# Two last products of a two-group matmul chain, each done in seven products of half the size

## The chip, the cores and the metric

The program runs on one core of a Trainium2 chip. The metric is the device time of one execution in microseconds (us). The core's engines work in parallel and are ordered by semaphores alone: TensorE (PE) multiplies, VectorE (DVE) and ScalarE (ACT) work element by element, GpSimd (POOL) and SyncE (SP) issue transfers here.

## The reference

For eight sequences of 256 tokens with 1024 features, one of eight square matrices is chosen for each sequence and applied; then a dense layer with a gated low-rank part is applied, and the input is added to the result:

```
xc  = einsum('bsi,boi->bso', x, weight[ids])             # 8 x 256 x 1024, one 1024 x 1024 matrix each
combine = top-2 of softmax(xc @ W_router.T), scaled to sum 1
h   = einsum('nd,erd->ner', xc, A_stack) * combine[..., None]
out = x + xc @ W_base.T + b_base + einsum('ner,eor->no', h, B_stack) * 2.0
```

## The kernel before, in words

**Two halves, high and low.** Each float32 operand is split in two fp32r values: ScalarE casts it (the high part, helper `hi`, line 492), VectorE subtracts the cast from the original (the low part, helper `lo`, line 553). A product is then three matmuls for each 128x128 block of weights (`product`, lines 813 to 815): high by high, high by low, low by high.

**Groups.** The sequences go in two groups of four. In each group the first part makes `xc` (`cond`, lines 828 and 832: 8 tiles of 128 outputs for a sequence). The second part multiplies all four sequences' `xc`, seen as a matrix of 1024 rows by 1024 tokens, by `W_base`. That product is done in seven products of half the size (P1, P2, P5, P6, P7, P4, P3, in this order in `second`), each of 512 outputs by 512 k by 512 tokens: four tiles m of 128 outputs, four k steps, three matmuls of 512 columns each. The sums that this needs of quarters of `W_base` (`s_sum`) and of `xc` (`t_sum`) are VectorE's (line 557), in place. P2, P7, P4 and P3 also take the low-rank part in (`lora_up`, three more matmuls to a tile).

**Banks and passes.** The eight accumulators are `bank_x0` to `bank_x3` and `bank_y0` to `bank_y3`. After a product VectorE adds a bank to the output in `out_sb` (`first_pass`, line 596; `last_pass`, line 604), and the next product goes on accumulating in the same bank; so TensorE waits for VectorE's pass of tile m before it writes the bank again (`wait_bank`, `cond_bank`). The output quarters are named t1/C11, t2/C12, t3/C22 and C21. P3 ends C12; it accumulates in `bank_y`, and in the second group its last tile is cut in two halves of 256 columns (`end_tile`, `end_passes`, line 612), so that the last pass and the last store are short.

**What sets the order.** Every engine has its own instruction list, written out by hand in program order, and does it strictly in that order. VectorE's list for the end of a group is in the loop over groups: passes, low parts for P3's weights, low parts of the next group's first `x` and `w` tiles. ScalarE's list is `base_splits`. SP issues the loads of `raw`'s six slots in a fixed order (`load_order`); each waits until the slot's former content has been used (`wait_free`), and what stands behind it waits too. POOL issues the loads of the residual `x` and all stores but the last.

## Time and profile before

| | us |
|---|---|
| median of 3 runs | 394.96 |
| lowest, highest | 394.69, 395.39 |
| the profiled execution's own time | 394.37 |
| its span, first to last instruction | 392.6 |

| engine | busy us | share of the span |
|---|---|---|
| TensorE matmul | 388.7 | 99% |
| TensorE weight load | 332.8 | 85% |
| VectorE | 302.0 | 77% |
| ScalarE | 183.6 | 47% |
| GpSimd | 50.0 | 13% |

A busy share tells how much of the span an engine had something to do. It is a mean over stages, and says nothing of the place where an engine is waited for. Of a matmul the profile gives start and a modelled duration that overlaps the next one; the pace is read from the distance of starts.

### The profile page before, as it was taken

The page shows a single profiled execution, that of the slowest core. Times are in us where ns is not written, and L with a number is a line of the kernel's source. Part 1 is how long each engine was busy: PE and PEld are TensorE (multiplying, and loading weights), DVE is VectorE, ACT ScalarE, POOL GpSimd, SP SyncE. Part 2 cuts the span into 40 slices and gives each one's busy share as a digit, 9 for nine tenths or more (in the row PEclk, how much of TensorE's full clock was granted, in tenths as well). Part 3 has the DMA queues.
Part 4 walks back from the last instruction along what each step waited for, and adds up shares of the span by engine and source line. Part 5 has one row for each costly group of instructions (what it writes and reads, how often), then busy time and mean ns, then how long its engine had stood idle before and what let it go on. Part 6 is the DMA issues. An engine that isn't in the chain of part 4 may idle for free.

```text
span 392.6 us, 5707 instructions
## 1 busy us (share of the span) xinstructions
PE 388.7 (99%) x2185; PEld 332.8 (85%) x2185; DVE 302.0 (77%) x431; ACT 183.6 (47%) x281; POOL 50.0 (13%) x84
## 2 busy tenths in 40 slices
PE   8999999999999999999999999999999999999997
PEld 8888888888888888888888888888888888888886
DVE  4897966789699999974458786778867989998322
ACT  5877734758632444232147666357656224441000
POOL 0101103110002130021130000260000202201110
PEclk9999999999999999999999999999999999999999
DMA  7997875869333145586668767489083302552222
GB/s 263 391 361 281 291 269 125 283 224 334 119 107 27 56 157 169 179 279 206 215 222 275 229 230 251 117 246 387 29 264 117 72 5 81 182 167 80 82 80 80
DMA packets 21979, 73.95 MB, mean 188 GB/s; under 512 B 3344, under 2 KB 3600, under 8 KB 21952
## 3 DMA queue, kind: packets, MB, share of 16 engines
q1 hardware_dynamic: 15984, 55.58, 41.5%
q0 software_dynamic: 5680, 16.96, 14.3%
q10 hardware_dynamic: 288, 1.05, 0.7%
q8 instruction: 17, 0.28, 0.3%
q14 instruction: 10, 0.08, 0.1%
HBM read 64.13 MB, written 8.39 MB: 185 GB/s over the span
## 4 chain that ended last, share of the span: by engine, by line
PE 99%; DVE 0%; issue 0%
PE bank_x L828 30%; PE bank_x L832 16%; PE bank_y L813 9%; PE bank_y L815 9%; PE bank_y L814 8%; PE bank_x L815 8%; PE bank_x L814 8%; PE bank_x L813 8%; PE bank_y L883 2%; PE bank_y L959 2%; DVE out_sb L612 0%; DVE h_hl L549 0%
## 5 line engine op out<-in xcount | busy, mean ns | idle before, releaser
L828 PE MATMUL bank_x<-x_hl,wc_hl 128*128 128x512 f32 x512 | 123.3, 391 | 0.0
L553 DVE TENSOR_TENSOR wc_hl<-raw,wc_hl 128x1024 fp32r<-128x1024 f32 x90 | 108.4, 1220 | 18.5 <-ACT wc_hl L492 18.3
L492 ACT CAST wc_hl<-raw 128x1024 fp32r<-128x1024 f32 x90 | 93.6, 1051 | 56.1 <-DVE raw L557 22.9
L828 PEld LDWEIGHTS bank_x<-x_hl,wc_hl 128*128 128x128 f32 x512 | 94.1, 189 | 18.0
L832 PEld LDWEIGHTS bank_x<-x_hl,wc_hl 128*128 128x128 f32 x512 | 65.9, 191 | 2.6
L832 PE MATMUL bank_x<-x_hl,wc_hl 128*128 128x256 f32 x512 | 66.7, 283 | 0.0
L521 ACT COPY xc_low<-bank_x 128x256 f32<-128x256 f32 x64 | 23.7, 370 | 33.7 <-PE bank_x L832 21.9
L706 DVE TENSOR_TENSOR xp<-bank_x,xc_low 128x256 f32<-128x256 f32 x64 | 26.9, 421 | 15.2 <-ACT xc_low L521 14.1
L814 PE MATMUL bank_x<-x_hl,wc_hl 128*128 128x512 f32 x96 | 37.4, 389 | 0.0
L815 PE MATMUL bank_x<-x_hl,wc_hl 128*128 128x512 f32 x96 | 37.4, 389 | 0.0
L813 PE MATMUL bank_x<-x_hl,wc_hl 128*128 128x512 f32 x96 | 37.4, 389 | 0.0
L526 ACT CAST xc_hl<-xp 128x256 fp32r<-128x256 f32 x64 | 26.0, 406 | 24.0 <-DVE xp L706 23.9
L596 DVE SCALAR_TENSOR_TENSOR out_sb<-bank_x,bias_sb,out_sb 128x512 f32<-128x512 f32 x32 | 23.6, 747 | 17.4 <-PE bank_x L815 15.1
L711 DVE TENSOR_TENSOR xc_hl<-xp,xc_hl 128x256 fp32r<-128x256 f32 x64 | 26.9, 420 | 7.5 <-ACT xc_hl L526 7.5
L431 POOL DMA_DIRECT2D out<-out_sb x28 | 15.4, 550 | 124.1 <-DVE out_sb L604 102.1
L425 POOL DMA_DIRECT2D out_sb<-x x32 | 22.9, 720 | 56.1 <-PE bank_x L828 55.9
L604 DVE TENSOR_TENSOR out_sb<-bank_y,out_sb 128x512 f32<-128x512 f32 x23 | 15.7, 688 | 15.1 <-PE bank_y L815 14.3
L440 POOL DMA_DIRECT2D gate_rows<-compared x16 | 9.6, 612 | 132.1 <-DVE compared L679 132.1
L492 ACT CAST x_hl<-xp 128x1024 fp32r<-128x1024 f32 x16 | 16.6, 1051 | 15.1 <-DVE xp L557 14.7
L814 PE MATMUL bank_y<-xc_hl,wc_hl 128*128 128x512 f32 x60 | 23.4, 389 | 0.0
L813 PE MATMUL bank_y<-xc_hl,wc_hl 128*128 128x512 f32 x60 | 23.4, 389 | 0.0
L815 PE MATMUL bank_y<-xc_hl,wc_hl 128*128 128x512 f32 x60 | 23.4, 389 | 0.0
(88 smaller groups left out, 505.5 us busy)
## 6 DMA issues: line engine op xcount, KB each, us to landing
raw<-w_cond SPq DMA_DIRECT2D x62, 512.0 KB, 4.7
raw<-w_base SPq DMA_DIRECT2D x24, 512.0 KB, 5.2
out_sb<-x POOLq DMA_DIRECT2D x32, 256.0 KB, 4.7
raw<-x SPq DMA_DIRECT2D x14, 512.0 KB, 4.8
out<-out_sb POOLq DMA_DIRECT2D x28, 256.0 KB, 2.3
raw<-x ACTq DMA_DIRECT2D x2, 512.0 KB, 3.7
raw<-w_cond SPq DMA_DIRECT2D x4, 256.0 KB, 3.5
gate_rows<-compared POOLq DMA_DIRECT2D x16, 64.0 KB, 3.9
```

The lines of the kernel that those rows point to most:

```text
L492: nc.scalar.copy(split_dst(key, HI), split_src(key)).then_inc(hi_done, 1)
L521: nc.scalar.copy(xc_low[:, t % 2], bank_x[t % HT][:, TOK:]).then_inc(low_copied, 1)
L526: nc.scalar.copy(xc_hl[:, t, HI, s % 2 * TOK:(s % 2 + 1) * TOK], xp[:, s // 2 % 2, t, s % 2 * TOK:(s % 2 + 1) * TOK]).then_inc(xc_hi, 1)
L553: nc.vector.tensor_tensor(split_dst(key, LO), split_src(key), split_dst(key, HI).bitcast(F32), ALU.subtract).then_inc(lo_done, 1)
L596: nc.vector.scalar_tensor_tensor(out_sb[:, o], bank_x[m][:], bias_sb[:, i:i + 1], out_sb[:, o], ALU.add, ALU.add).then_inc(pass_done, 1)
L706: nc.vector.tensor_tensor(xc, bank_x[t % HT][:, 0:TOK], xc_low[:, t % 2], ALU.add) \
L711: nc.vector.tensor_tensor(xc_hl[:, t, LO, s % 2 * TOK:(s % 2 + 1) * TOK], xc, xc_hl[:, t, HI, s % 2 * TOK:(s % 2 + 1) * TOK].bitcast(F32), ...
L813: nc.tensor.matmul(ps, w_hi, v_hi, start=start, stop=False, skip_group_check=resumed)
L814: nc.tensor.matmul(ps, w_hi, v_lo, start=False, stop=False, skip_group_check=resumed)
L815: return nc.tensor.matmul(ps, w_lo, v_hi, start=False, stop=stop, skip_group_check=resumed)
L828: return nc.tensor.matmul(ps[:], wc_hl[:, slot_of(s, t), HI, k], x_hl[:, s % 2, k].rearrange("p h n -> p (h n)"), start=(k == 0), stop=stop)
L832: return nc.tensor.matmul(ps[:, TOK:], wc_hl[:, slot_of(s, t), LO, k], x_hl[:, s % 2, k, HI], start=False, stop=stop)
```

## The change

In both groups P3 is itself done in seven products of 256 outputs by 256 k by 256 tokens. They are called P1 to P7 again, with their operands U (weights) and V (`xc`); TensorE does them in `third` in the order P1, Y, P6, P5, P7, P3, P4. A tile of one has two k steps and three matmuls each, all of 256 columns, and each of the seven has two tiles; P2's two tiles are the first part of Y0 and Y1. Y0 to Y3 are the low-rank part of the four tiles of C12 (three matmuls of 512 columns each, as before). P1, P6, P7 and P4 accumulate in `bank_x0/1`, P5 and P3 in `bank_x2/3`, Y in `bank_y`.

VectorE makes four sums for U and four for V (`u_sum`, `v_sum`, 512 elements to a partition each), the low parts of seven U and four V (512 elements each; three V are quarters of an operand that is split already), and adds every stage's bank to C12 (`inner_passed`: twelve passes of 256 columns, four of 512). ScalarE makes the eleven high parts. The low and high parts of P3's weights (two of 1024 elements each) go, and so do P3's four passes of 512 columns and `end_tile`. The new list of VectorE is `last_stages`. The next group's first matmuls wait for the passes of the inner P4 and P3 now, and before waited for those of C21; the loads of two `raw` slots for the next group's third and fourth `w` tiles wait for inner sums and splits.

The diff, cut to its core:

```diff
+INNER = [(P1, "t1"), ("Y", "Y"), (P6, "t2"), (P5, "C22"), (P7, "t3"), (P3, "C12"), (P4, "C21")]
+INNER_TILES = [(j, m) for j, _ in INNER for m in range(HT if j == "Y" else HT // 2)]
+INNER_W = {P1: (0, 0), P2: (0, 1), P4: (1, 1)}
+INNER_X = {P1: (0, 0), P2: (1, 0), P3: (1, 1)}
+U_SUMS, V_SUMS = (P5, P6, P7, P3), (P5, P6, P7, P4)
+U_PLACE = (P1, P2, P6, P5, P7, P3, P4)
...
-            P7: s(P4), P4: s(P3) + ([] if last else [("x", n, 0), ("x", n, 1)]),
-            P3: [] if last else [("w", n, 0), ("w", n, 1), ("w", n, 2), ("w", n, 3)]}
+            P7: s(P4),
+            P4: [("U", g, P1), ("U", g, P2)] + ([] if last else [("x", n, 0), ("x", n, 1)]) +
+                [("V", g, P6), ("U", g, P6), ("V", g, P5), ("U", g, P5), ("V", g, P7)],
+            P3: [("U", g, P7), ("U", g, P3), ("V", g, P4), ("U", g, P4)] +
+                ([] if last else [("w", n, 0), ("w", n, 1), ("w", n, 2), ("w", n, 3)])}
...
+        def w_quarter(r, c):
+            return raw[:, R1 + r].rearrange("p (m k n) -> p m k n", m=2, k=HT)[:, :, 2 * c:2 * c + 2]
+        def x_quarter(r, c):
+            return xp[:, 1, HT + 2 * r:HT + 2 * r + 2, c * TOK:(c + 1) * TOK]
...
-                elif kind in ("A11", "A12", "A22", "A22b"):
-                    j = {"A11": P7, "A12": P2, "A22": P3, "A22b": P4}[kind]
+                elif kind == "A22":
+                    sp.wait_ge(summed, SUM["U", g, P3])
+                    sp.wait_ge(lo_done, SPLIT["U", g, P4 if h else P2])
+                elif kind in ("A11", "A12", "A22b"):
...
+                if kind == "U":
+                    q = U_PLACE.index(j)
+                    act.wait_ge(product_done, made(i, P7, q // 2 * 2 + 1) if q < 4 else made(i, P4, HT - 1))
+                if kind == "V":
+                    act.wait_ge(product_done, made(i, P7, HT - 1))
...
+            def u_sum(g, j):
+                dve.wait_ge(summed, SUM["U", g, {P6: P5, P3: P6}[j]] if j in (P6, P3) else SUM["S", g, (P3, 1)])
+                a, b, op = {P5: (w_quarter(1, 0), w_quarter(1, 1), ALU.add),
+                            P6: (u_plain(P5), w_quarter(0, 0), ALU.subtract),
+                            P7: (w_quarter(0, 0), w_quarter(1, 0), ALU.subtract),
+                            P3: (w_quarter(0, 1), u_plain(P6), ALU.subtract)}[j]
+                total(u_plain(j), a, b, op)
+            def v_sum(g, j):
+                if j in (P6, P4):
+                    dve.wait_ge(summed, SUM["V", g, {P6: P5, P4: P6}[j]])
+                a, b = {P5: (x_quarter(0, 1), x_quarter(0, 0)), P6: (x_quarter(1, 1), v_plain(P5)),
+                        P7: (x_quarter(1, 1), x_quarter(0, 1)), P4: (x_quarter(1, 0), v_plain(P6))}[j]
+                total(v_plain(j), a, b, ALU.subtract)
...
+            def inner_passed(g, j, m):
+                o = OUT_SLOT["C12"]
+                if (j, m) in ((P1, 0), (P1, 1), ("Y", 2), ("Y", 3)):
+                    dve.wait_ge(pass_done, passed(g, "t2", m))
+                else:
+                    dve.wait_ge(inner_pass, {"Y": inner(g, P1, m % 2), P6: inner(g, "Y", m % 2),
+                                             P5: inner(g, "Y", 2 + m % 2), P7: inner(g, P5, m % 2),
+                                             P3: inner(g, P6, m % 2), P4: inner(g, "Y", 2 + m % 2)}[j])
+                dve.wait_ge(inner_done, inner(g, j, m))
+                if j == "Y":
+                    dst, ps = out_sb[:, o + m], bank_y[m][:]
+                else:
+                    c = 0 if j in (P1, P4) else TOK
+                    dst = out_sb[:, o + m + (0 if j in (P1, P6, P3) else 2), c:c + TOK]
+                    ps = bank_x[m + (2 if j in (P5, P3) else 0)][:, 0:TOK]
+                nc.vector.tensor_tensor(dst, ps, dst, ALU.add).then_inc(inner_pass, 1)
+            def last_stages(g):
+                def los(*keys):
+                    for key in keys:
+                        lo(key)
+                n = GSEQS * (g + 1)
+                last = g == GROUPS - 1
+                los(("U", g, P1))
+                first_pass(g, "t3", 3)
+                last_pass(g, "C22", 3)
+                los(("U", g, P2))
+                first_pass(g, "C21", 0)
+                if not last:
+                    los(("x", n, 0), ("x", n, 1))
...
+                if not last:
+                    los(("w", n, 1))
+                for m in range(2):
+                    inner_passed(g, P7, m)
+                for m in range(2):
+                    inner_passed(g, P3, m)
+                if not last:
+                    los(("w", n, 2))
+                for m in range(2):
+                    inner_passed(g, P4, m)
+                if not last:
+                    los(("w", n, 3))
...
-                        pe.wait_ge(pass_done, passed(s // GSEQS - 1, "C21", t))
+                        pe.wait_ge(inner_pass, inner(s // GSEQS - 1, P4 if t < 2 else P3, t % 2))
...
+            def inner_tile(g, j, m, ps, resumed):
+                pe.wait_ge(lo_done, SPLIT["U", g, j])
+                if j not in INNER_X:
+                    pe.wait_ge(lo_done, SPLIT["V", g, j])
+                for k in range(2):
+                    mm = product(ps, u_split(g, j, HI)[:, m, k], u_split(g, j, LO)[:, m, k], v_split(j, HI)[:, k],
+                                 v_split(j, LO)[:, k], not resumed and k == 0, k == 1, resumed=resumed)
+                return mm
+            def third(g):
+                for j, m in INNER_TILES:
+                    if j == "Y":
+                        pe.wait_ge(pass_done, passed(g, "C22", m))
+                        if m < 2:
+                            inner_tile(g, P2, m, bank_y[m][:, 0:TOK], True)
+                        mm = lora_up(bank_y[m][:], KT + m, 1)
+                    else:
+                        b = m + (2 if j in (P5, P3) else 0)
+                        if j in (P1, P5):
+                            pe.wait_ge(pass_done, passed(g, "C21", b))
+                        else:
+                            pe.wait_ge(inner_pass, inner(g, {P6: P1, P7: P6, P4: P7, P3: P5}[j], m))
+                        mm = inner_tile(g, j, m, bank_x[b][:, 0:TOK], j not in (P1, P5))
+                    mm.then_inc(inner_done, 1)
```

VectorE's list from the end of P7 to the end of group 0, before (L553 low parts, L596 and L604 passes; the rows of `x_hl` and the last rows of `wc_hl` are the next group's):

```order
L553 TENSOR_TENSOR wc_hl<-raw,wc_hl 128x1024 [waits hi_done]
L596 SCALAR_TENSOR_TENSOR out_sb<-bank_x0,bias_sb,out_sb 128x512 [waits res_in0,product_done]
L553 TENSOR_TENSOR x_hl<-raw,x_hl 128x4x256 [waits hi_done] x2
L596 SCALAR_TENSOR_TENSOR out_sb<-bank_x1,bias_sb,out_sb 128x512 [waits res_in1,product_done]
L596 SCALAR_TENSOR_TENSOR out_sb<-bank_x2,bias_sb,out_sb 128x512 [waits res_in2,product_done]
L596 SCALAR_TENSOR_TENSOR out_sb<-bank_x3,bias_sb,out_sb 128x512 [waits res_in3,product_done]
L553 TENSOR_TENSOR wc_hl<-raw,wc_hl 128x1024 [waits hi_done] x2
L604 TENSOR_TENSOR out_sb<-bank_y0,out_sb 128x512 [waits pass_done,product_done]
L604 TENSOR_TENSOR out_sb<-bank_y1,out_sb 128x512 [waits pass_done,product_done]
L553 TENSOR_TENSOR wc_hl<-raw,wc_hl 128x1024 [waits hi_done]
L604 TENSOR_TENSOR out_sb<-bank_y2,out_sb 128x512 [waits pass_done,product_done]
L604 TENSOR_TENSOR out_sb<-bank_y3,out_sb 128x512 [waits pass_done,product_done]
```

The same place now, its first twelve rows (L627 are sums, L623 low parts, L666 C21's passes; `xp` holds the new sums):

```order
L666 SCALAR_TENSOR_TENSOR out_sb<-bank_x0,bias_sb,out_sb 128x512 [waits res_in0,product_done]
L623 TENSOR_TENSOR x_hl<-raw,x_hl 128x4x256 [waits hi_done] x2
L627 TENSOR_TENSOR xp<-xp 128x512
L627 TENSOR_TENSOR xp<-xp 128x512 [waits summed]
L627 TENSOR_TENSOR xp<-raw 128x512 [waits summed]
L627 TENSOR_TENSOR xp<-xp,raw 128x512 [waits summed]
L666 SCALAR_TENSOR_TENSOR out_sb<-bank_x1,bias_sb,out_sb 128x512 [waits res_in1,product_done]
L623 TENSOR_TENSOR x_hl<-xp,x_hl 128x512 [waits hi_done]
L623 TENSOR_TENSOR wc_hl<-xp,wc_hl 128x512 [waits hi_done]
L627 TENSOR_TENSOR xp<-xp 128x512
L627 TENSOR_TENSOR xp<-xp 128x512 [waits summed]
L666 SCALAR_TENSOR_TENSOR out_sb<-bank_x2,bias_sb,out_sb 128x512 [waits res_in2,product_done]
```

Between two of C21's passes, where nothing or one low part stood, there are now three to six instructions.

The end of VectorE's list for group 0 now (L709 are `inner_passed`; the rows of `wc_hl` with 1024 elements are the next group's weights; the first `bank_x0/1` pair is P7's, the second P4's, `bank_x2/3` are P5's and P3's):

```order
L623 TENSOR_TENSOR wc_hl<-raw,wc_hl 128x1024 [waits hi_done]
L709 TENSOR_TENSOR out_sb<-bank_x2,out_sb 128x256 [waits inner_done,inner_pass]
L709 TENSOR_TENSOR out_sb<-bank_x3,out_sb 128x256 [waits inner_done,inner_pass]
L623 TENSOR_TENSOR wc_hl<-raw,wc_hl 128x1024 [waits hi_done]
L709 TENSOR_TENSOR out_sb<-bank_x0,out_sb 128x256 [waits inner_done,inner_pass]
L709 TENSOR_TENSOR out_sb<-bank_x1,out_sb 128x256 [waits inner_done,inner_pass]
L709 TENSOR_TENSOR out_sb<-bank_x2,out_sb 128x256 [waits inner_done,inner_pass]
L709 TENSOR_TENSOR out_sb<-bank_x3,out_sb 128x256 [waits inner_done,inner_pass]
L623 TENSOR_TENSOR wc_hl<-raw,wc_hl 128x1024 [waits hi_done]
L709 TENSOR_TENSOR out_sb<-bank_x0,out_sb 128x256 [waits inner_done,inner_pass]
L709 TENSOR_TENSOR out_sb<-bank_x1,out_sb 128x256 [waits inner_done,inner_pass]
L623 TENSOR_TENSOR wc_hl<-raw,wc_hl 128x1024 [waits hi_done]
```

The four low parts of the next group's weights stand between the inner passes, three of them ahead of P4's.

TensorE's list at the boundary of P4 and P3 in group 0, before:

```order
L813 MATMUL bank_x3<-h_hl,b_hl 128x512
L814 MATMUL bank_x3<-h_hl,b_hl 128x512
L815 MATMUL bank_x3<-h_hl,b_hl 128x512
L813 MATMUL bank_y0<-xc_hl,wc_hl 128x512 [waits pass_done,lo_done]
L814 MATMUL bank_y0<-xc_hl,wc_hl 128x512
L815 MATMUL bank_y0<-xc_hl,wc_hl 128x512
L813 MATMUL bank_y0<-xc_hl,wc_hl 128x512
L814 MATMUL bank_y0<-xc_hl,wc_hl 128x512
L815 MATMUL bank_y0<-xc_hl,wc_hl 128x512
```

TensorE's list at the boundary of group 0 and group 1, now (L933 to L935 are the inner P4, L948 and L952 the next group's first tiles):

```order
L933 MATMUL bank_x1<-x_hl,xc_hl 128x256 [waits lo_done,inner_pass]
L934 MATMUL bank_x1<-x_hl,xc_hl 128x256
L935 MATMUL bank_x1<-x_hl,xc_hl 128x256
L933 MATMUL bank_x1<-x_hl,xc_hl 128x256
L934 MATMUL bank_x1<-x_hl,xc_hl 128x256
L935 MATMUL bank_x1<-x_hl,xc_hl 128x256
L948 MATMUL bank_x0<-x_hl,wc_hl 128x512 [waits lo_done,inner_pass,hi_done]
L948 MATMUL bank_x0<-x_hl,wc_hl 128x512 x7
L948 MATMUL bank_x1<-x_hl,wc_hl 128x512 [waits inner_pass,hi_done]
L952 MATMUL bank_x0<-x_hl,wc_hl 128x256 [waits lo_done]
L952 MATMUL bank_x0<-x_hl,wc_hl 128x256 x7
```

The tile that follows P3 on TensorE now waits for `inner_pass`, a pass of the product just done, where it waited for passes of C21 that had been done a stage earlier.

## Rows read from the trace of the kernel before

**Rows 1.** The page: busy time, and the chain that ended last.

```profile
PE 388.7 (99%) x2185; PEld 332.8 (85%) x2185; DVE 302.0 (77%) x431; ACT 183.6 (47%) x281; POOL 50.0 (13%) x84
PE 99%; DVE 0%; issue 0%
```

**Rows 2.** Windows of group 0's P4 and P3: us, busy us of each engine (instructions).

```profile
171.10:184.70 13.60, 13.60 (x61) 11.27 (x60) 7.09 (x8) 4.01 (x4) 2.17 (x4) 1.00 0.81 290
184.70:198.30 13.60, 13.60 (x61) 11.27 (x60) 6.32 (x7) 2.10 (x2) 2.16 (x4) 1.00 0.58 194
```

**Rows 3.** Timeline, PE: start us, us, what; group 1's P3, then group 0's end.

```profile
375.93 0.39 PE L813 MATMUL bank_y<-xc_hl,wc_hl 128*128 128x512 f32 x1
...
386.13 0.28 PE L813 MATMUL bank_x<-xc_hl,wc_hl 128*128 128x256 f32 x1
...
389.60 0.28 PE L815 MATMUL bank_x<-h_hl,b_hl 128*128 128x256 f32 x1
...
198.33 0.84 PE L828 MATMUL bank_x<-x_hl,wc_hl 128*128 128x512 f32 x3
```

**Rows 4.** Timeline, DVE, group 0's P4 and P3 ([idle before it <- ended by]).

```profile
172.79 1.22 DVE L553 TENSOR_TENSOR wc_hl<-raw,wc_hl 128x1024 fp32r<-128x1024 f32 x1
174.73 0.75 DVE L596 SCALAR_TENSOR_TENSOR out_sb<-bank_x,bias_sb,out_sb 128x512 f32<-128x512 f32 x1 [0.72 <-PE bank_x L815]
175.39 2.35 DVE L553 TENSOR_TENSOR x_hl<-raw,x_hl 128x1024 fp32r<-128x1024 f32 x2
178.13 0.75 DVE L596 SCALAR_TENSOR_TENSOR out_sb<-bank_x,bias_sb,out_sb 128x512 f32<-128x512 f32 x1 [0.38 <-PE bank_x L815]
181.53 0.75 DVE L596 SCALAR_TENSOR_TENSOR out_sb<-bank_x,bias_sb,out_sb 128x512 f32<-128x512 f32 x1 [2.65 <-PE bank_x L815]
184.93 0.75 DVE L596 SCALAR_TENSOR_TENSOR out_sb<-bank_x,bias_sb,out_sb 128x512 f32<-128x512 f32 x1 [2.65 <-PE bank_x L815]
...
198.53 0.69 DVE L604 TENSOR_TENSOR out_sb<-bank_y,out_sb 128x512 f32<-128x512 f32 x1 [2.71 <-PE bank_y L815]
```

**Rows 5.** Timeline, DVE, a busy stretch of group 0's P2: independent instructions.

```profile
132.03 1.28 DVE L604 TENSOR_TENSOR out_sb<-bank_y,out_sb 128x512 f32<-128x512 f32 x2
133.23 2.35 DVE L557 TENSOR_TENSOR xp<-xp 128x1024 f32<-128x1024 f32 x2
135.50 0.68 DVE L604 TENSOR_TENSOR out_sb<-bank_y,out_sb 128x512 f32<-128x512 f32 x1
```

**Rows 6.** Timeline, DVE: two passes of P1, then the next instruction.

```profile
125.51 1.40 DVE L596 SCALAR_TENSOR_TENSOR out_sb<-bank_x,bias_sb,out_sb 128x512 f32<-128x512 f32 x2
126.83 0.68 DVE L618 TENSOR_TENSOR h_sb<-h_sb,gate_rows 128x512 f32<-128x512 f32 x1
```

**Rows 7.** Timeline, DVE, 256 elements: a dependent pair, then an independent pair.

```profile
115.50 0.43 DVE L662 TENSOR_TENSOR compared<-compared,const_sb 128x256 f32<-128x256 f32 x1
115.97 0.43 DVE L664 TENSOR_TENSOR compared<-compared 128x256 f32<-128x256 f32 x1
...
211.05 0.41 DVE L706 TENSOR_TENSOR xp<-bank_x,xc_low 128x256 f32<-128x256 f32 x1
211.39 1.21 DVE L553 TENSOR_TENSOR wc_hl<-raw,wc_hl 128x1024 fp32r<-128x1024 f32 x1
```

**Rows 8.** Groups by line and shape: busy us, mean ns; idle before, releaser.

```profile
L553 DVE TENSOR_TENSOR xc_hl<-xp,xc_hl 128x1024 fp32r<-128x1024 f32 x8 | 9.4, 1220 | 0.0
L496 ACT CAST h_hl<-h_sb 128x512 fp32r<-128x512 f32 x4 | 2.5, 621 | 16.5 <-DVE h_sb L618 16.5
```

**Rows 9.** Line 394 (SP's loads of `raw`): the time to landing.

```profile
DMA to landing us min/median/max: 3.2/4.9/9.1
```

**Rows 10.** Timeline, DVE, group 1's P4 and P3.

```profile
365.93 0.75 DVE L596 SCALAR_TENSOR_TENSOR out_sb<-bank_x,bias_sb,out_sb 128x512 f32<-128x512 f32 x1 [0.72 <-PE bank_x L815]
...
376.13 0.75 DVE L596 SCALAR_TENSOR_TENSOR out_sb<-bank_x,bias_sb,out_sb 128x512 f32<-128x512 f32 x1 [2.65 <-PE bank_x L815]
...
389.92 0.42 DVE L612 TENSOR_TENSOR out_sb<-bank_x,out_sb 128x256 f32<-128x256 f32 x1 [1.30 <-PE bank_x L815]
```

**Rows 11.** The program's start: PE timeline (the warm-up's last ten matmuls), and the page's clock.

```profile
4.78 2.33 PE L959 MATMUL bank_y<-h_hl 128*128 128x256 f32 x10
...
PEclk9999999999999999999999999999999999999999
```

More of the change, by code:

```diff
@@ L191 @@
 PASSES = [("t1", m) for m in range(HT)] + [("C11", m) for m in range(HT)] + [("t2", m) for m in range(HT)] + \
-    [(c, m) for m in range(HT) for c in ("t3", "C22")] + [("C21", m) for m in range(HT)] + \
-    [("C12", m) for m in range(HT)]
+    [(c, m) for m in range(HT) for c in ("t3", "C22")] + [("C21", m) for m in range(HT)]
 def passed(g, c, m):
@@ L285, in build @@
         stored = [sem(f"stored{i}") for i in range(OUTS)]
-        end_clear = sem("end_clear")
-        end_done = sem("end_done")
-        end_pass = sem("end_pass")
-        end_stored = [sem(f"end_stored{m}") for m in range(HT - 1 + len(END))]
+        inner_done = sem("inner_done")
+        inner_pass = sem("inner_pass")
+        end_stored = [sem(f"end_stored{n}") for n in range(6)]
         block = ctx.enter_context(nc.Block())
@@ L329, in split_src @@
             kind, i, j = key
+            if kind in ("U", "V"):
+                return u_plain(j) if kind == "U" else v_plain(j)
             if kind == "T":
@@ L395, in _ @@
                 in_slot[slot] = key
-            g = GROUPS - 1
-            for m in range(HT - 1):
-                sp.wait_ge(pass_done, passed(g, "C12", m))
-                nc.sync.dma_start(out[2 * g + 1, m], out_sb[:, OUT_SLOT["C12"] + m]).then_inc(end_stored[m], 16)
-            m = HT - 1
-            for n, (a, b) in enumerate(END):
-                sp.wait_ge(end_pass, n + 1)
-                nc.sync.dma_start(out[2 * g + 1, m, :, a:b], out_sb[:, OUT_SLOT["C12"] + m, a:b]) \
-                    .then_inc(end_stored[m + n], 16)
+            g, o = GROUPS - 1, OUT_SLOT["C12"]
+            ends = [(P7, 0, 2, TOK, PTOK), (P7, 1, 3, TOK, PTOK), (P3, 0, 0, 0, PTOK), (P3, 1, 1, 0, PTOK),
+                    (P4, 0, 2, 0, TOK), (P4, 1, 3, 0, TOK)]
+            for n, (j, i, m, a, b) in enumerate(ends):
+                sp.wait_ge(inner_pass, inner(g, j, i))
+                nc.sync.dma_start(out[2 * g + 1, m, :, a:b], out_sb[:, o + m, a:b]).then_inc(end_stored[n], 16)
             for o in range(OUTS):
@@ L477, in hi @@
                     act.wait_ge(raw_in[slot], landed)
+                elif kind == "U":
+                    act.wait_ge(summed, SUM["S", i, (P3, 1)])
                 elif kind != "T":
@@ L490, in hi @@
                 if kind == "w" and i and i % GSEQS == 0 and j < 4:
-                    act.wait_ge(product_done, made(i // GSEQS - 1, P4 if j < 2 else P3, 2 * (j % 2) + 1))
+                    before = i // GSEQS - 1
+                    if j < 2:
+                        act.wait_ge(product_done, made(before, P4, 2 * j + 1))
+                    else:
+                        act.wait_ge(inner_done, inner(before, "Y", 1) if j == 2 else inner(before, P5, 1))
                 nc.scalar.copy(split_dst(key, HI), split_src(key)).then_inc(hi_done, 1)
@@ new lines, in last_stages @@
+            def last_stages(g):
[11 more added lines that the diff above has]
+                    los(("x", n, 0), ("x", n, 1))
+                v_sum(g, P5)
+                v_sum(g, P6)
+                u_sum(g, P5)
+                u_sum(g, P6)
+                first_pass(g, "C21", 1)
+                los(("V", g, P6), ("U", g, P6))
+                v_sum(g, P7)
+                v_sum(g, P4)
+                first_pass(g, "C21", 2)
+                u_sum(g, P7)
+                u_sum(g, P3)
+                los(("V", g, P5), ("U", g, P5))
+                first_pass(g, "C21", 3)
+                los(("V", g, P7))
+                for m in range(2):
+                    inner_passed(g, P1, m)
+                los(("U", g, P7), ("U", g, P3))
+                for m in range(HT):
+                    inner_passed(g, "Y", m)
+                los(("V", g, P4), ("U", g, P4))
+                for m in range(2):
+                    inner_passed(g, P6, m)
+                if not last:
+                    los(("w", n, 0))
+                for m in range(2):
+                    inner_passed(g, P5, m)
+                if not last:
+                    los(("w", n, 1))
+                for m in range(2):
+                    inner_passed(g, P7, m)
+                for m in range(2):
+                    inner_passed(g, P3, m)
+                if not last:
+                    los(("w", n, 2))
+                for m in range(2):
+                    inner_passed(g, P4, m)
+                if not last:
+                    los(("w", n, 3))
@@ L877, in router @@
                 if p == 2:
-                    pe.wait_ge(pass_done, passed(0, "C12", HT - 1))
+                    pe.wait_ge(inner_pass, inner(0, "Y", 1))
                 for k in range(KT):
```

106 lines of the change are left out of this document (43 added, 63 removed).

## The prediction

> **What bounds the kernel now.** First the page: TensorE is busy 99% of the span, the chain that ended last is 99% TensorE, and VectorE is busy 77% [rows 1]. Then the windows of the two stages that the change rewrites in group 0: TensorE fills both, 13.60 us each, and VectorE works 7.09 and 6.32 us in them [rows 2]. So 13.79 of 27.2 us are free on VectorE, and the question is whether what the change puts there fits, in the written order. The timeline of VectorE shows where its free time lies: every pass from 174.73 on starts when TensorE delivers, with up to 2.65 us of idle time ahead [rows 4]. TensorE's starts give the paces: from 375.93 to 386.13 it starts 45 matmuls of 512 columns, 0.2267 us each; from 386.13 the 30th of 256 columns starts at 389.60, 29 steps of 0.1197, call it 0.120 us [rows 3]. The second is more than half of the first; a matmul of half the columns is not half price.
>
> **TensorE's work.** Before, P3 takes 48 matmuls of 512 columns and 12 for the low-rank part. Now there are seven products of two tiles, two k steps and three matmuls: 84 of 256 columns, and the same 12.
> - Group 0: 84 x 0.120 = 10.08 in place of 48 x 0.2267 = 10.88 us. Saved: 0.80 us, if TensorE is never made to wait.
> - Group 1, where the last tile is in 256 columns already: before 45 x 0.2267 + 30 x 0.120 = 13.80, now 84 x 0.120 + 12 x 0.2267 = 12.80 us. Saved: 1.00 us.
>
> The new matmuls read other tiles than those of rows 3, but have their form and weight load. The bounds: no cheaper than 0.1197; at the dearest each as dear as a whole row of 0.2267, which nothing suggests. I take 0.120.
> The Trainium skill ("TensorE: Matmul & The Clock Gate", Back-to-back issue gap) gives N/2.4 + 2.5 ns, an estimate of 0.109 and 0.216 us. By it group 1 would save 1.23 us, not 1.00; the trace's paces are both 0.011 us above it, and the trace decides.
>
> **VectorE's prices.** Independent instructions of 512 elements start 0.60 apart (132.03 to 133.23 for two), of 1024 elements 1.135 (133.23 to 135.50 for two) [rows 5]; C21's kind of pass takes 0.66 (125.51 to 126.83 for two) [rows 6]. With 256 elements one follows 0.34 after an independent one, and 0.47 after one that it needs [rows 7]: a dependence adds 0.13. The new sums read with strides. Bounds: as cheap as 0.60, or 0.73 with the dependence's spacing each. Low parts with strided operands take 1220 ns, like the contiguous ones [rows 8, 4]; so 0.60.
>
> **Group 0, VectorE's list from 174.73.** Up to there nothing moves: P7's last pass and the low part at 172.79 (now half as long) are ahead of C21's first pass, which waits for TensorE [rows 4]. From then to the pass of inner P4's first tile the list has:
> - four passes of C21, 4 x 0.66 = 2.64
> - low parts of the next group's `x`, 2 x 1.13 = 2.26
> - 21 of 512 elements: eight sums, nine low parts, four passes Y; 21 x 0.60 = 12.60, and 2 x 0.13 as two sums need the one just ahead
> - ten inner passes of 256, 3.40
> - low parts of three `w` tiles, 3 x 1.135 = 3.40
>
> Together 24.56 us. With no gap this puts P4's first pass at 199.29. Is there no gap? TensorE's inputs to it are early: from 184.73 (13.60 ahead of 198.33, rows 3) P1 ends at 186.2, Y at 190.3, P6 and P5 at 193.2, while VectorE comes to their passes at 187.7, 189.6, 193.2 and 195.0. P7 then waits 0.4 us for P6's pass and P4 a little for P7's, and P4's first tile is ready at about 198.2. ScalarE's casts of 512 elements take 0.62 [rows 8]; the tightest is U of P6: summed at 180.4, cast by 181.1, wanted at 181.6. The `w` tile whose slot the last sum frees (185.3) lands 4.9 us later, at worst 9.1 [rows 9], so it is cast by 195.5, wanted at 198.15. The next slot is freed at 193.3, and SP's later loads stand behind it; they land about 200, wanted after 203. So VectorE's list is closed, and it sets the end.
> TensorE's first matmul of the next group needs that pass: 199.29 + 0.42 + 0.05 = 199.76, where it started at 198.33 [rows 3]. Group 0 loses 1.43 us; its 0.80 us are turned into waits. Nothing gives that back: behind it TensorE is full to the end. What is late next is the last `w` low part (about 201), wanted by TensorE at 207.
>
> **Group 1.** The same list without the 2.26 and the four `w` low parts. From 365.93 it reaches C21's last pass at 376.1, where TensorE delivers it [rows 10]. Y's passes start from 379.2 and then follow TensorE, which from 375.93 is at 377.4 after P1, 381.5 after Y, 384.4 after P5. P6's pass is over at 384, before P7 wants it. No wait: the full 1.00 us. The last pass moves from 389.92 [rows 10] to 388.92. Behind it is as before a store of 256 columns; the four stores ahead of it are 0.72 us apart now. Cost between 0 and 0.3 us of landing; I take 0.
>
> **Sum.** +1.43 - 1.00 = +0.43 us. The profiled execution took 394.37 us, a span of 392.6 and 1.8 around it, 0.59 under the median of 394.96. It becomes 394.80, the median 395.39. A measurement of this kernel can tell about 0.2%, 0.79 us, from no change.
>
> **Rivals.**
> - *VectorE doesn't bind, faster.* If the inner passes come in time, both savings stand: -1.80 us, 393.2. For it: VectorE had 13.79 us free, and the list adds about as much (11 low parts and 8 sums of 0.60, twelve passes of 0.34, less two low parts of 1.13: 13.2). Against: 1.3 us of the free time is ahead of 174.73, and the next group's weights stand ahead of P4's passes. To save anything the 24.56 must shrink below 23.
> - *VectorE's instructions don't close up, slower.* Each pays the dependence's 0.13 where it reads what was just made elsewhere: nine low parts and the four Y passes, 1.7 us, 397.1. It decides from 0.36 us more on the list. For it: rows 7; most of these wait for a semaphore. Against: low parts that wait for one and find it given follow at the independent pace (175.39, two in 2.35) [rows 4]. If every one started only when the one ahead has ended (0.68, 0.43, 0.75, 1.22), the list would be 27.8 us and the time 398.6. The Trainium skill says so ("VectorE: DVE Perf Modes", The DRAIN you can't avoid: the next operation doesn't start before the pipe is empty). Rows 5 speak against it: two of 0.68 take 1.28 together.
> - *TensorE's clock falls in the new waits, slower.* The first matmuls of the program, 256 columns, take 0.23 us each, the 1.2 GHz level, though the page's granted clock reads 9 there too [rows 11]; later ones 0.120. If the waits at 193 to 199.7 brought it back for one pair of tiles, 16 matmuls of each width, that would be +5.5 us, 401. The waits are short and the trace shows none in mid-program, so little speaks for it.
> - *A weight tile lands late* is covered by 2.6 us even at 9.1 us, and counts for nothing.
>
> **How the numbers follow.** The forecast, 395.4, has a chance of 0.53, with a range of its own from 394.9 to 396.2; 0.08 of it is above 0.2%, as gaps only add. VectorE not binding, whole or in part: 0.18, all of it faster. Instructions not closing up, in part or whole: 0.24, slower. The clock: 0.05. So faster 0.18, same 0.45, slower 0.37. The range reaches from 394.0 (most of the first rival is left out, 0.12) to 397.2 (the clock and the case of 398.6 are left out, 0.08).
>
> **What would show it.** In VectorE's timeline of group 0: no idle time from 174.7 to P4's passes at about 199.3, and the first wide matmul of the next group at about 199.8, released by VectorE's inner pass. TensorE idle between the inner products of group 0, not of group 1. Group 1's TensorE from the start of P3 to the last matmul 12.8 us instead of 13.8, its last pass 1.0 us earlier against the start of that stage. Wrong it would be if VectorE's 512-element instructions start other than 0.60 apart, if the 256-column matmuls start other than 0.12 apart, or if the next group starts on time.

## The result

| | us |
|---|---|
| kernel before, median of 11 runs | 394.78 (394.38 to 395.39) |
| changed kernel, median of 11 runs | 395.88 (395.58 to 396.79) |
| ratio | 1.0032, 95% interval 1.0023 to 1.0040 |
| profiled execution of the changed kernel | 396.25, span 394.5 |

The change makes the kernel 1.1 us slower by the medians, 0.9 to 1.6 by the interval. The forecast was +0.43 us, a time of 395.4: right in direction and with 395.88 inside its own band of 394.9 to 396.2, but the change is 2.6 times as large. More than 0.2% slower, as it came out, had been given a chance of 0.37, and "same" 0.45.

The page of the changed kernel, against [rows 1]:

```profile
PE 387.6 (98%) x2242; PEld 333.1 (84%) x2242; DVE 327.8 (83%) x487; ACT 192.0 (49%) x299; POOL 49.9 (13%) x84
PE 91%; DVE 5%; issue 1%; DMA 1%; SPq 1%; ACT 0%; DVEq 0%; ACTq 0%
```

TensorE has 1.1 us less to do and is a smaller part of the chain that ended last; 5% of it are VectorE's now. The windows of the same two stages, against [rows 2] (the second ends where the next group starts):

```profile
171.66:185.26 13.60, 13.60 (x61) 11.26 (x60) 11.94 (x18) 2.91 (x5) 1.79 (x4) 1.00 0.26 101
185.26:200.30 15.04, 13.76 (x97) 12.40 (x95) 15.04 (x29) 6.20 (x8) 1.99 (x4) 1.00 0.52 188
```

In the second VectorE is busy 15.04 of 15.04 us, TensorE 13.76. VectorE's timeline there, against [rows 4]:

```profile
175.29 0.75 DVE L666 SCALAR_TENSOR_TENSOR out_sb<-bank_x,bias_sb,out_sb 128x512 f32<-128x512 f32 x1 [1.26 <-PE bank_x L935]
175.96 2.35 DVE L623 TENSOR_TENSOR x_hl<-raw,x_hl 128x1024 fp32r<-128x1024 f32 x2
178.23 1.42 DVE L627 TENSOR_TENSOR xp<-xp 128x512 f32<-128x512 f32 x2
179.56 0.68 DVE L627 TENSOR_TENSOR xp<-raw 128x512 f32<-128x512 f32 x1
...
181.55 0.68 DVE L623 TENSOR_TENSOR x_hl<-xp,x_hl 128x512 fp32r<-128x512 f32 x1
182.15 0.68 DVE L623 TENSOR_TENSOR wc_hl<-xp,wc_hl 128x512 fp32r<-128x512 f32 x1
182.75 1.29 DVE L627 TENSOR_TENSOR xp<-xp 128x512 f32<-128x512 f32 x2
...
190.15 2.48 DVE L709 TENSOR_TENSOR out_sb<-bank_y,out_sb 128x512 f32<-128x512 f32 x4
...
198.66 1.22 DVE L623 TENSOR_TENSOR wc_hl<-raw,wc_hl 128x1024 fp32r<-128x1024 f32 x1
199.80 0.75 DVE L709 TENSOR_TENSOR out_sb<-bank_x,out_sb 128x256 f32<-128x256 f32 x2
```

The first row is C21's first pass; no row behind it has an idle time. The last is inner P4's first pass, 24.51 us later. And TensorE, against [rows 3]: a wait inside the product, and the next group's first matmul.

```profile
194.22 0.38 PE L933 MATMUL bank_x<-x_hl,xc_hl 128*128 128x256 f32 x1 [0.27 <-DVE out_sb L709]
194.44 0.28 PE L934 MATMUL bank_x<-x_hl,xc_hl 128*128 128x256 f32 x1
...
200.36 2.33 PE L948 MATMUL bank_x<-x_hl,wc_hl 128*128 128x512 f32 x9 [0.86 <-DVE out_sb L709]
```

**Where the time went.** The absolute starts can't be compared at once: the first tiles start at another time in every execution, as the first weights land. So four landmarks are read: T0, the start of the second row of 16 narrow matmuls (256 columns) in the chain that ended last (`--critical`); T1, the start of such a row in the next group; the start of the last pass; the end of the span. In the kernel before T0 and T1 are

```profile
20.45 1.91 PE bank_x L832 x16
...
206.09 1.91 PE bank_x L832 x16
```

and in the changed kernel

```profile
21.01 1.91 PE bank_x L952 x16
...
208.25 1.91 PE bank_x L952 x16
```

All kernels of this study, in us. The three middle columns are of the profiled executions; the third is good to 0.05 only, as the page gives the span to 0.1. "Before, same runs" is the kernel before, measured together with that kernel.

| kernel | T0 to T1 | T1 to last pass | last pass to end | median | before, same runs |
|---|---|---|---|---|---|
| before | 185.64 | 183.83 | 2.68 | | |
| changed | 187.24 | 182.91 | 3.34 | 395.88 | 394.78 |
| e1 group 0 only | 187.17 | 183.83 | 2.66 | 396.20 | 394.80 |
| e2 group 1 only | 185.68 | 182.91 | 2.63 | 393.70 | 394.80 |
| e3 `w` last | 185.59 | 182.92 | 3.31 | 394.66 | 394.80 |
| e4 early halves | 187.22 | 182.92 | 2.81 | 395.23 | 394.80 |
| e5 changed, 24 memsets | 187.19 | 182.92 | 2.63 | 395.29 | 394.74 |
| e6 group 1 only, 29 memsets | 185.62 | 182.92 | 2.64 | 393.91 | 394.74 |
| e7 `x` early, `w` last | 185.07 | 182.92 | 3.20 | 393.60 | 394.74 |
| e8 `x` early | 186.50 | 182.91 | 3.33 | 395.24 | 394.74 |
| e9 group 1 only, 41 memsets | 185.64 | 182.92 | 3.05 | 394.43 | 394.81 |
| e10 as e7, 24 memsets | 185.09 | 182.91 | 2.80 | 393.21 | 394.81 |
| e11 as e10, early halves | 185.08 | 182.91 | 2.65 | 393.18 | 394.81 |

The changed kernel against before: +1.60 in group 0 and into the next (T0 to T1), -0.92 in group 1, +0.66 behind the last pass, together +1.34 (the medians differ by 1.10, with an interval that reaches from 0.9 to 1.6). The rest of the spans' 1.9 us is T0, 0.56 later; T0 lies between 20.3 and 21.3 in all these kernels and goes with none of the edits.

The third term was not in the prediction. Line 461 are SP's stores; the changed kernel's last passes and issues are

```profile
389.01 0.42 DVE L709 TENSOR_TENSOR out_sb<-bank_x,out_sb 128x256 f32<-128x256 f32 x1 [0.29 <-PE bank_x L935]
390.10 0.78 DVE L709 TENSOR_TENSOR out_sb<-bank_x,out_sb 128x256 f32<-128x256 f32 x2 [0.66 <-PE bank_x L935]
391.16 0.42 DVE L709 TENSOR_TENSOR out_sb<-bank_x,out_sb 128x256 f32<-128x256 f32 x1 [0.29 <-PE bank_x L935]
...
L461 SPq DMA_DIRECT2D out<-out_sb x6: 332/444/936, 388.0 to 391.7; - x6
DMA to landing us min/median/max: 2.3/2.6/3.0
```

The passes come 0.72 us apart, but the third last starts at 390.10 and not at 389.73; an issue takes up to 936 ns, where it took 332 to 347 before; a store lands after 2.3 to 3.0 us, where it was 1.7 to 2.0. The long issue starts at 388.74, before the late pass; the two will turn out to be different things.

### The profile page after: what moved, and what is told of

Same layout as the page of the kernel before. It is cut to its first block, busy times and chain, and to the rows that moved or that the text cites. A ratio compares the mean times of both kernels' runs of the same rounds, so it can differ in the third digit from the quotient of the medians.

```text
span 394.5 us, 5965 instructions
## 1 busy us (share of the span) xinstructions
PE 387.6 (98%) x2242; PEld 333.1 (84%) x2242; DVE 327.8 (83%) x487; ACT 192.0 (49%) x299; POOL 49.9 (13%) x84
## 3 DMA queue, kind: packets, MB, share of 16 engines
q10 hardware_dynamic: 288, 1.05, 0.7%
## 4 chain that ended last, share of the span: by engine, by line
PE 91%; DVE 5%; issue 1%; DMA 1%; SPq 1%; ACT 0%; DVEq 0%; ACTq 0%
PE bank_x L948 30%; PE bank_x L952 16%; PE bank_x L933 8%; PE bank_x L935 8%; PE bank_x L934 8%; PE bank_y L933 7%; PE bank_y L934 7%; PE bank_y L935 7%; PE bank_y L1003 2%; DVE xp L627 1%; DVE out_sb L709 1%; DVE x_hl L623 1%; DMA raw<-w_cond 1%; DVE wc_hl L623 1%; SPq L420 1%
## 5 line engine op out<-in xcount | busy, mean ns | idle before, releaser
L948 PE MATMUL bank_x<-x_hl,wc_hl 128*128 128x512 f32 x512 | 123.8, 392 | 1.8 <-ACT wc_hl L580 0.9
L623 DVE TENSOR_TENSOR wc_hl<-raw,wc_hl 128x1024 fp32r<-128x1024 f32 (+1 forms) x90 | 106.3, 1196 | 17.8 <-ACT wc_hl L562 17.6
L948 PEld LDWEIGHTS bank_x<-x_hl,wc_hl 128*128 128x128 f32 x512 | 93.7, 188 | 20.6 <-ACT wc_hl L580 1.5
L562 ACT CAST wc_hl<-raw 128x1024 fp32r<-128x1024 f32 (+1 forms) x90 | 91.5, 1031 | 34.0 <-DVE raw L627 25.2
L952 PEld LDWEIGHTS bank_x<-x_hl,wc_hl 128*128 128x128 f32 x512 | 65.9, 191 | 2.7
L952 PE MATMUL bank_x<-x_hl,wc_hl 128*128 128x256 f32 x512 | 66.7, 283 | 0.0
L934 PE MATMUL bank_x<-x_hl,wc_hl 128*128 128x512 f32 (+1 forms) x112 | 41.9, 374 | 0.0
L935 PE MATMUL bank_x<-x_hl,wc_hl 128*128 128x512 f32 (+1 forms) x112 | 41.9, 374 | 0.0
L933 PE MATMUL bank_x<-x_hl,wc_hl 128*128 128x512 f32 (+1 forms) x112 | 41.9, 374 | 0.0
L562 ACT CAST x_hl<-xp 128x1024 fp32r<-128x1024 f32 (+1 forms) x24 | 21.6, 908 | 36.4 <-DVE xp L627 36.1
L596 ACT CAST xc_hl<-xp 128x256 fp32r<-128x256 f32 x64 | 26.0, 406 | 23.6 <-DVE xp L856 23.4
L666 DVE SCALAR_TENSOR_TENSOR out_sb<-bank_x,bias_sb,out_sb 128x512 f32<-128x512 f32 x32 | 23.5, 746 | 6.5 <-PE bank_y L935 3.5
L623 DVE TENSOR_TENSOR x_hl<-xp,x_hl 128x1024 fp32r<-128x1024 f32 (+1 forms) x24 | 24.5, 1040 | 1.6 <-ACT x_hl L562 1.6
L934 PEld LDWEIGHTS bank_x<-x_hl,wc_hl 128*128 128x128 f32 x112 | 21.1, 188 | 3.9
L933 PEld LDWEIGHTS bank_x<-x_hl,wc_hl 128*128 128x128 f32 x112 | 21.1, 188 | 3.8
L935 PEld LDWEIGHTS bank_x<-x_hl,wc_hl 128*128 128x128 f32 x112 | 21.1, 188 | 3.7
```

The costliest lines, as they stand in the source:

```text
L562: nc.scalar.copy(split_dst(key, HI), split_src(key)).then_inc(hi_done, 1)
L596: nc.scalar.copy(xc_hl[:, t, HI, s % 2 * TOK:(s % 2 + 1) * TOK], xp[:, s // 2 % 2, t, s % 2 * TOK:(s % 2 + 1) * TOK]).then_inc(xc_hi, 1)
L623: nc.vector.tensor_tensor(split_dst(key, LO), split_src(key), split_dst(key, HI).bitcast(F32), ALU.subtract).then_inc(lo_done, 1)
L666: nc.vector.scalar_tensor_tensor(out_sb[:, o], bank_x[m][:], bias_sb[:, i:i + 1], out_sb[:, o], ALU.add, ALU.add).then_inc(pass_done, 1)
L933: nc.tensor.matmul(ps, w_hi, v_hi, start=start, stop=False, skip_group_check=resumed)
L934: nc.tensor.matmul(ps, w_hi, v_lo, start=False, stop=False, skip_group_check=resumed)
```

## Experiments

**e1, e2: the change in one group.**

The diff against the changed kernel, cut (e2 has `(1,)`). A group that isn't in `IN_GROUPS` has the lists, waits and stores of the kernel before.

```diff
+IN_GROUPS = (0,)
...
+                if g in IN_GROUPS:
+                    last_stages(g)
+                    continue
...
-                third(g)
+                if g in IN_GROUPS:
+                    third(g)
+                else:
+                    second(g, P3)
```

> The change in group 0 only; group 1 does its P3 as before. Theory (VectorE's list sets the start of the next group; the trace of the changed kernel has the next group's first tile 1.59 us late against the same point counted from the program's first tiles): +1.6 us on the kernel before, about 396.4, and TensorE's first wide matmul of group 1 starts after VectorE's pass of inner P4, 1.4 to 1.6 us late. Rival A (the loss is spread over both groups, or comes with the later start of 0.57 us seen in the one trace): +0.6 to +0.8, about 395.5. Rival B (VectorE doesn't bind): -0.8, 394.0.

> The change in group 1 only; group 0 does its P3 as before. Theory (0.91 us saved on TensorE, 0.66 us lost after the last pass because the last six stores crowd): -0.25 us, about 394.5, with 2.9 us between the last pass and the end. Rival A (the tail's 0.66 us is chance of the one trace): -0.9, about 393.9. Rival B (the start 0.57 us later belongs to the change): +0.3, about 395.1.

Measured: e1 396.20, ratio 1.0035 (1.0022 to 1.0049), +1.4 us, T0 to T1 +1.53 and nothing else (183.83 and 2.66 as before): the theory. e2 393.70, ratio 0.9968 (0.9956 to 0.9981), -1.1 us: not the theory but its rival A, for behind the last pass 2.63 us passed as before. But the changed kernel's 0.66 us are no chance: e3 and e8 have them too. The two parts together make +0.3, the whole made +1.1. Something costs only where both are there.

**e3: the next group's `w` low parts behind P4's passes.**

```diff
-                if not last:
-                    los(("w", n, 0))
...
-                if not last:
-                    los(("w", n, 1))
...
-                if not last:
-                    los(("w", n, 2))
                 for m in range(2):
                     inner_passed(g, P4, m)
                 if not last:
-                    los(("w", n, 3))
+                    los(("w", n, 0), ("w", n, 1), ("w", n, 2), ("w", n, 3))
```

> The changed kernel with the low parts of the next group's four weight tiles moved behind the passes of inner P4 in group 0. Theory (VectorE's list is the bound): 3.4 us leave the list ahead of P4's passes, TensorE then has only the 0.4 us before P7 to wait, group 0 costs -0.3 instead of +1.6: about 1.9 us faster than the changed kernel, 394.0, 0.8 under the kernel before. Rival A (the sums and low parts inside the product bind TensorE, not those weights): no change, 395.9. Rival B (the moved low parts are late for the next group's first tiles): a wait of 0.5 to 1 us at its second tile, 394.7.

Measured: 394.66, ratio 0.9991 (0.9982 to 1.0000), 1.2 us under the changed kernel. T0 to T1 fell by 1.65 us: VectorE's list was the bound. TensorE then starts the next group at 198.98, 177.70 from T0, 0.18 earlier than before (0.3 was expected). The time is 0.7 us above the 394.0 of the theory and at the 394.7 of rival B, but rival B's wait isn't there: behind the moved work TensorE has no idle time up to T1. The theory reckoned the 1.9 us from landmarks of one execution of the changed kernel, +1.34 against before, where the medians differ by 1.10, and it left out the spacing of the first wide matmuls (below).

**e4: stores of the two halves that are final early.**

```diff
-            ends = [(P7, 0, 2, TOK, PTOK), (P7, 1, 3, TOK, PTOK), (P3, 0, 0, 0, PTOK), (P3, 1, 1, 0, PTOK),
+            ends = [("Y", 0, 0, 0, TOK), ("Y", 1, 1, 0, TOK), (P7, 0, 2, TOK, PTOK), (P7, 1, 3, TOK, PTOK),
+                    (P3, 0, 0, TOK, PTOK), (P3, 1, 1, TOK, PTOK),
                     (P4, 0, 2, 0, TOK), (P4, 1, 3, 0, TOK)]
```

> The changed kernel with the left halves of C12's tiles 0 and 1 stored as soon as they are final (after Y0 and Y1), so that the last stores are six of 128 KB, 0.72 us apart, and not two of 256 KB among them; eight stores in all. Theory (the last stores crowd on the DMA engines, busy 0.97 in the last stretch): 0.4 to 0.6 us faster than the changed kernel, 395.4, with 2.3 to 2.5 us from last pass to end. Rival (the time is SP's, in issuing: its last issues take 0.44 us in the median, at most 0.94): two more issues, no gain or 0.1 slower, 395.9.

Measured: 395.23, 0.65 under the changed kernel, and 2.81 us behind the last pass, where 2.3 to 2.5 were expected. The bytes play a part. The late pass stayed (0.66 idle ahead of it, as above), which stores alone don't explain, and an issue still takes 0.81 us.

**e5, e6, e9: VectorE's program in another place.** The page counts pieces of program fetched by DMA: q14 has 10 in the kernel before, in e1 and in e2, and 11 in the changed kernel, in e3, e4 and e8. Cut by time, the eleventh is moved at 390.9 us, right there. One-element memsets in VectorE's idle time shift it (the diff of e5, cut):

```diff
+        idle_pad = sb("idle_pad", [P, 64])
...
                         split(late_splits(s, t))
+                        if s == 1 and t < KT - 1:
+                            for i in range(5 * t, min(5 * t + 5, 24)):
+                                nc.vector.memset(idle_pad[:, i:i + 1], 0.0)
```

e6 is e2 with 29 of them, e9 e2 with 41.

> The changed kernel with 24 one-element memsets on VectorE, in its idle time in group 0's second sequence. They compute nothing; they only move the places in VectorE's program at which a piece of it is fetched. Theory (the changed kernel has one more instruction fetch, on q14, at 390.8 us, between its last passes, where the third last pass starts 0.37 us late and SP's last issues take up to 0.94 us instead of 0.33; the kernel with the change in group 1 alone has none there and no loss): no fetch in the last passes, 2.6 to 2.7 us from last pass to end instead of 3.34, 0.6 to 0.7 us faster than the changed kernel, 395.2. Rival (the last stores' crowding alone, or another engine's program): unchanged, 395.9.

> The change in group 1 only, with 29 such memsets on VectorE, so that VectorE's program has as many instructions before its last passes as the changed kernel's. Theory (VectorE's instruction fetch): the fetch falls between the last passes here too, the last pass-to-end time grows from 2.63 to about 3.3 us, 0.5 to 0.7 us slower than without, 394.3. Rival (TensorE's program or group 0's work is what brings the loss): unchanged, 393.7.

> The change in group 1 only, with 41 one-element memsets on VectorE in idle time instead of 29: counted with its pure waits, VectorE's program then has 584 instructions, as the changed kernel's (543 without; with 29 it had 572, and no fetch fell in the last passes). Theory (VectorE's instruction fetch among the last passes and stores costs the 0.6 us): an eleventh fetch on q14 between the last passes, the third last pass 0.37 us late, SP's issues up to 0.9 us, 3.3 us from last pass to end instead of 2.63: 394.4, 0.6 over the kernel with the change in group 1 only. Rival (the crowd of stores needs something of group 0 or of TensorE's longer program): 2.63 us stay, 393.8.

Measured, e5: 395.29, 0.6 under the changed kernel, with more instructions than it. The piece is moved at 381.6 us, and a pass of Y starts late there instead (380.97; the row ahead of it holds two that start 0.60 apart, so 380.82 was due). The last passes are 0.72 apart again, and 2.63 us lie behind the last:

```profile
379.62 1.28 DVE L624 TENSOR_TENSOR xc_hl<-xp,xc_hl 128x512 fp32r<-128x512 f32 x2
380.97 0.69 DVE L710 TENSOR_TENSOR out_sb<-bank_y,out_sb 128x512 f32<-128x512 f32 x1
...
389.13 0.42 DVE L710 TENSOR_TENSOR out_sb<-bank_x,out_sb 128x256 f32<-128x256 f32 x1 [0.30 <-PE bank_x L939]
389.85 0.42 DVE L710 TENSOR_TENSOR out_sb<-bank_x,out_sb 128x256 f32<-128x256 f32 x1 [0.29 <-PE bank_x L939]
390.57 0.42 DVE L710 TENSOR_TENSOR out_sb<-bank_x,out_sb 128x256 f32<-128x256 f32 x1 [0.29 <-PE bank_x L939]
...
L462 SPq DMA_DIRECT2D out<-out_sb x6: 332/340/727, 387.4 to 391.0; - x6
DMA to landing us min/median/max: 1.7/2.1/2.2
```

e6 missed: 393.91 and 2.64 us, no eleventh fetch. The 29 were counted without the pure waits for semaphores, which are instructions too; with them 12 were still wanting. e9 has these 12, and the fetch comes, at 389.1 us:

```profile
387.88 0.78 DVE L725 TENSOR_TENSOR out_sb<-bank_x,out_sb 128x256 f32<-128x256 f32 x2 [0.67 <-PE bank_x L997]
388.95 0.43 DVE L725 TENSOR_TENSOR out_sb<-bank_x,out_sb 128x256 f32<-128x256 f32 x1 [0.29 <-PE bank_x L997]
...
q14 instruction: 11, 0.09, 0.1%
...
DMA to landing us min/median/max: 1.7/2.3/2.5
```

The third last pass is late by the same 0.37 us, though that kernel's group 0 and TensorE's program are those of e2; 3.05 us lie behind the last pass (3.3 were expected), and no issue takes over 0.43 us (0.9 were expected); 394.43, 0.7 over e2 and 0.5 over e6. Twelve memsets in idle time do it. This is the term that only both groups together had: each adds about 40 instructions to VectorE's program (502 records in the trace of the kernel before, 543 in e1, 541 in e2, 582 in the changed kernel and in e9), and a certain place in it is met among the last passes.

The traces show that place. In all nine kernels whose list is long enough the 576th record of VectorE, waits counted, starts 0.43 to 0.44 us behind the record of its wait, where the passes beside it start 0.07 behind. It is the third last pass in the changed kernel, e3, e4, e7, e8 and e9, and with 24 memsets more it is a pass of Y (380.97 in e5), where nobody waits for it at the end. The piece itself is moved 0.6 to 1.2 us after that start, so the pass isn't waiting for this piece to land.

SP's long issues are another matter, though the expectations of e5 and e9 put them down to the same fetch. They go with a piece on q8, which by its count goes with TensorE's program (17 pieces in the kernel before and with the change in group 1, 18 with it in group 0 or both). It is moved at 388.0 us in the changed kernel, 3.2 us ahead of the last pass, and the issue of 936 ns starts at 388.74. e5 and e10 have that piece 3.5 and 3.2 us ahead of the last pass and the long issue too, without a piece of VectorE's there; e10:

```profile
L462 SPq DMA_DIRECT2D out<-out_sb x6: 332/390/1049, 385.6 to 389.2; - x6
```

Sorted by what is fetched in the last 4 us ahead of the last pass or beside it:

| fetched there | kernels | longest issue of SP's last stores, us | last pass to end, us |
|---|---|---|---|
| nothing | before, e1, e2, e6 | 0.35 | 2.63 to 2.68 |
| TensorE's piece | e5, e10, e11 | 0.55 to 1.05 | 2.63 to 2.80 |
| VectorE's piece | e9 | 0.43 | 3.05 |
| both | changed, e3, e7, e8 | 0.82 to 1.01 | 3.20 to 3.34 |
| both, halves stored early | e4 | 0.81 | 2.81 |

So VectorE's piece costs 0.4 us alone, TensorE's at most 0.2, and the two together 0.5 to 0.7. Whether the two only add up or make each other worse can't be told from one profiled execution of each kernel, and no run has TensorE's piece shifted by itself.

**e7, e8: the next group's `x` low parts in VectorE's idle times ahead of C21.**

```diff
                 los(("U", g, P1))
+                if not last:
+                    los(("x", n, 0))
                 first_pass(g, "t3", 3)
                 last_pass(g, "C22", 3)
                 los(("U", g, P2))
-                first_pass(g, "C21", 0)
                 if not last:
-                    los(("x", n, 0), ("x", n, 1))
+                    los(("x", n, 1))
+                first_pass(g, "C21", 0)
```

The list of ScalarE's casts is put in the same order (not shown). e8 is this alone, e7 this with e3's edit.

> The changed kernel with the low parts of the next group's `x` moved into VectorE's two idle times ahead of 174.73 and those of its `w` behind inner P4's passes; VectorE's list ahead of that pass is 5.66 us shorter. Theory (VectorE's list is the bound of group 0): TensorE isn't made to wait inside the product, group 0 saves the full 0.8 us, the next group starts 0.8 us early instead of 1.43 late: 2.2 to 2.4 us under the changed kernel, 393.6. Rival (what group 0 loses is TensorE's own, in 256-column matmuls): like the kernel with the `w` low parts last, 394.7.

> The changed kernel with the low parts of the next group's `x` alone moved ahead. Theory: the list is 2.26 us shorter, P4's first pass at 197.0 and TensorE free at 197.5 both ahead of 198.33, so the next group starts 0.6 to 0.8 us early: 2.0 to 2.3 us under the changed kernel, 393.8, and 0.8 to 0.9 faster than with the `w` low parts last, though less work left the list ahead of P4, because there P6's passes came late for P7. Rival (only the sum of VectorE's work ahead of P4's pass counts, so that 3.4 us moved beat 2.26): slower than with `w` last, 394.9 or more.

Measured: e7 393.60, ratio 0.9972 (0.9963 to 0.9981), the theory. The chain that ended last is 99% TensorE again. The next group starts at 197.69, 177.18 from T0, 0.70 earlier than before, and T0 to T1 is 0.57 shorter, where 0.8 was expected. The rest is in the handing over: the pass that the next group needs lasts from 197.12 to 197.54, so that the next group starts 0.24 us behind TensorE's last narrow matmul (197.45) and not 0.12, and its first nine wide matmuls take 2.32 us where they took 2.20.

```profile
197.69 2.32 PE L944 MATMUL bank_x<-x_hl,wc_hl 128*128 128x512 f32 x9
```

e8 came to 395.24, 0.64 under the changed kernel and not the 2.1 expected: the time is the rival's (394.9 or more). Its list has idle times in the middle:

```profile
185.68 0.75 DVE L666 SCALAR_TENSOR_TENSOR out_sb<-bank_x,bias_sb,out_sb 128x512 f32<-128x512 f32 x1 [0.25 <-PE bank_x L937]
...
190.00 2.06 DVE L709 TENSOR_TENSOR out_sb<-bank_y,out_sb 128x512 f32<-128x512 f32 x3 [0.51 <-PE bank_y L937]
191.98 0.68 DVE L623 TENSOR_TENSOR x_hl<-xp,x_hl 128x512 fp32r<-128x512 f32 x1
...
199.24 0.75 DVE L709 TENSOR_TENSOR out_sb<-bank_x,out_sb 128x256 f32<-128x256 f32 x2
```

With 2.26 us less ahead of it VectorE catches up with TensorE at C21's last two passes and at Y, and waits. From Y's last pass on it still has 7.9 us to do before P4's pass, three `w` low parts among it, and that piece alone now sets the end. So the rival's reason, a mere sum, isn't it either: the list starts anew wherever it has to wait.

**e10, e11: the parts together.** e10 is e7 with 24 memsets, e11 this with e4's stores.

> The kernel with the next group's `x` low parts early and `w` low parts last, and 24 memsets on VectorE. Theory: the two losses are separate and both gone: 0.7 us gained in group 0, 0.9 in group 1, no fetch in the tail: 393.0, 1.7 under the kernel before. Rival: the fetch's cost hides elsewhere, as 393.6 without the memsets.

> The same, with the left halves of tiles 0 and 1 of C12 stored early. Theory (without the fetch the crowd of the last stores costs little: last pass to end 2.63 against 2.68 before): 0 to 0.2 us less, 392.9. Rival (the 0.65 us that the early halves gave the changed kernel is the crowd's own): 392.4.

Measured: e10 393.21, ratio 0.9958 (0.9944 to 0.9972), 1.6 us under the kernel before: the losses are separate and go separately. e11 393.18: the early halves give next to nothing once VectorE's piece isn't fetched in the tail (2.65 us behind the last pass against 2.80). That their 0.65 us in e4 came from a crowd of fetches and stores together is what this suggests; it isn't shown by itself.

## Why the prediction was right or wrong

- **VectorE's prices and list, group 0: right.** Forecast were 24.56 us from C21's first pass to P4's first; measured 24.51 (175.29 to 199.80). New strided forms start 0.60 apart (181.55 to 182.15), a needed predecessor adds 0.13 (178.23: two in 1.42, where independent ones take 1.29). No term of the list stands in for another: the sum was right because its parts were. The Trainium skill ("VectorE: DVE Perf Modes", The DRAIN you can't avoid) has the next operation start only when the pipe is empty, and adds that an operation which isn't held back starts earlier; here, as in the trace of before, the next starts ahead of the end of the one before. The price of that rival was summed a little high: with the durations given, the list is 27.7 us and not 27.8.
- **The start of the next group: nearly right.** +1.43 forecast. From T0 it starts 1.47 us later (200.36 - 21.01 against 198.33 - 20.45), and T1 is 1.60 later: the first matmuls behind the wait are spaced wider, nine wide ones in 2.33 us where they took 2.20, and at 194.22 the next starts 0.22 after and not 0.12. That restart was left out. It doesn't grow with the wait: behind the wait of about 0.1 us in e7 the nine take 2.32.
- **TensorE's work: right.** Group 1 forecast -1.00; measured -0.92 in all kernels with the change there. From the start of P3 to the start of the last matmul it is 12.70 us (378.08 to 390.78), where it was 13.67 (375.93 to 389.60), so 0.97 were saved; the last pass starts 0.38 behind the last matmul and not 0.32. The 256-column matmuls start 0.12 apart. The estimate of 0.109 us from the Trainium skill's formula ("TensorE: Matmul & The Clock Gate", Back-to-back issue gap) doesn't hold here.
- **"Behind it is as before a store of 256 columns; I take 0": this term failed.** It was mis-sized: 0.66 us, outside the bounds of 0 to 0.3 that were given. The stores alone cost nothing (2.63 us in e2, with the same six). A fetch of VectorE's program fell among them, for 0.4 us in e9, where nothing else is fetched, and 0.7 between e5 and the changed kernel, which both have TensorE's fetch too. No rival had it: the rows of before were read for what instructions do, never for how they come.
- **Rivals.** That VectorE doesn't bind, that its instructions don't close up, and that the clock falls, all fell; the granted clock is 1.00 in the window with the waits, and the matmuls behind them keep 0.12.
- Taken together: +1.60 - 0.92 + 0.66 = +1.34 by landmarks, +1.43 - 1.00 + 0 forecast. Of the missing 0.91 us 0.66 are the tail, 0.17 the start of the next group (0.04) and the restart behind it (0.13), 0.08 group 1. That 395.88 still lies in the band of 394.9 to 396.2 is luck as far as the tail goes: the band's upper part was left for gaps in VectorE's list, and there were none.
